# The mean of the feed-forward weights' magnitudes, taken in the course of the loop and applied in the out phase

## What is computed

```
def binarize_weight(W):
    alpha = jnp.mean(jnp.abs(W), axis=tuple(range(1, W.ndim)), keepdims=True)
    return alpha * jnp.sign(W)

xn = _layernorm(x)
ffn = einsum('bsi,oi->bso', xn, binarize_weight(weight_real)) + bias
attn: qkv = clip(xn @ Wqkv.T, -8, 8); q, k layer-normed with weights and biases;
      32 heads of 32, scores + ALiBi slopes, causal softmax, @ v, @ Wout.T
return x + attn + ffn
```

## Time and profile before

| what | value |
|---|---|
| median of 3 runs | 1423.8 us (1423.53 to 1425.67) |
| the profiled execution's own time | 1431.37 us |
| its span | 1429.6 us |
| mean granted TensorE clock | 0.987 |
| TensorE busy | 94% |
| VectorE, ScalarE, GpSimd busy | 55%, 36%, 29% |

### The profile page before, as it was taken

How to read it: one execution, slowest core, us unless ns; L and a number is a source line. 1 busy time by engine, 2 the same in 40 slices (tenths; PEclk the granted TensorE clock), 3 DMA queues, 4 the chain that set the end, 5 groups by cost and what they waited for, 6 DMA issues and landing times.

```text
span 1429.6 us, 36331 instructions
## 1 busy us (share of the span) xinstructions
PE 1347.4 (94%) x15016; PEld 680.6 (48%) x15016; DVE 789.9 (55%) x1790; ACT 511.0 (36%) x1018; POOL 421.2 (29%) x300
## 2 busy tenths in 40 slices
PE   3899999999999999699999999999999999879998
PEld 2455444454544444244345555555555555434443
DVE  7566266565666661122678778878778778001111
ACT  4454111111111110000057777777777777600000
POOL 5222000000000000000015555444455555545443
PEclk9899999999999999899999999999999999989999
DMA  6454122322223226522112322333223331225543
GB/s 241 155 168 148 74 52 66 74 73 66 67 66 73 66 71 154 168 84 71 56 51 75 88 79 79 92 85 91 83 78 88 85 85 48 91 67 162 152 157 118
DMA packets 143653, 137.47 MB, mean 96 GB/s; under 512 B 81952, under 2 KB 110752, under 8 KB 143328
## 3 DMA queue, kind: packets, MB, share of 16 engines
q1 hardware_dynamic: 79053, 99.02, 23.3%
q10 hardware_dynamic: 64467, 36.50, 9.7%
HBM read 92.90 MB, written 42.21 MB: 95 GB/s over the span
## 4 chain that ended last, share of the span: by engine, by line
PE 79%; DMA 10%; DVE 6%; SPq 2%; issue 1%; POOL 1%; ACT 1%; DVEq 0%; ACTq 0%; POOLq 0%
PE ps L1004 52%; PE ps L1079 6%; PE ps L1140 6%; DMA arena<-arena 6%; PE ps L1163 5%; PE ps L1168 4%; DVE ps L907 2%; PE ps L1056 2%; DMA arena<-q_scr 2%; PE ps L1143 1%; DMA r_scr<-arena 1%; SPq L353 1%; PE ps L1173 1%; DVE arena L835 1%; PE ps L993 1%
## 5 line engine op out<-in xcount | busy, mean ns | idle before, releaser
L1004 PE MATMUL ps<-arena 128*128 128x512 f16 x3584 | 796.0, 382 | 31.8 <-DVE arena L866 11.9
L1004 PEld LDWEIGHTS ps<-arena 128*128 128x128 f16 (+1 forms) x3584 | 349.6, 98 | 453.4 <-issue 20.5
L723 ACT ACTIVATE arena<-ps 128x512 f32<-128x512 f32 (+3 forms) x768 | 339.6, 498 | 151.1 <-PE ps L1143 98.4
L599 POOL TENSOR_TENSOR arena<-arena 128x2048 f32<-128x2048 f32 (+1 forms) x48 | 201.8, 4204 | 391.0 <-ACT arena L723 388.6
L907 DVE CUSTOM_DVE_ANT_0 ps<-ps,arena 128x128 f32<-128x128 f32 (+3 forms) x512 | 239.6, 519 | 59.1 <-PE ps L1079 57.0
L1140 PE MATMUL ps<-arena 128*32 128x512 f16 (+3 forms) x3072 | 255.5, 327 | 4.0 <-ACT arena L723 2.5
L1079 PE MATMUL ps<-arena 127*32 127x512 f16 (+3 forms) x3072 | 237.2, 327 | 17.3 <-DVE arena L907 12.8
L638 ACT ACTIVATE arena<-arena 128x512 f32 (+1 forms) x64 | 40.1, 628 | 486.7 <-DMA arena<-in_wqkv_t 313.7
L866 DVE TENSOR_SCALAR arena<-ps 128x1024 f32<-128x1024 f32 x48 | 58.8, 1225 | 218.5 <-PE ps L1004 189.2
L911 DVE TENSOR_REDUCE arena<-ps 128x1 f16<-128x512 f32 x256 | 162.9, 683 | 15.2 <-PE ps L1079 15.2
L1163 PE MATMUL ps<-arena 128*32 128x512 f32 (+3 forms) x1536 | 160.7, 485 | 0.5 <-issue 0.3
(11 more groups left out here) (51 smaller groups left out, 769.2 us busy)
## 6 DMA issues: line engine op xcount, KB each, us to landing
arena<-in_x SPq DMA_DIRECT2D x32, 512.0 KB, 4.9
arena<-in_wqkv_t SPq DMA_DIRECT2D x48, 256.0 KB, 3.0
arena<-k_scr ACTq DMA_DIRECT2D x39, 256.0 KB
base_scr<-arena SPq DMA_DIRECT2D x16, 512.0 KB, 2.8
v_scr<-arena SPq DMA_DIRECT2D x16, 512.0 KB, 2.9
arena<-r_scr SPq DMA_DIRECT2D x32, 256.0 KB
arena<-base_scr SPq DMA_DIRECT2D x16, 512.0 KB, 4.0
out_dram<-arena SPq DMA_DIRECT2D x16, 512.0 KB, 6.2
```

The lines of the kernel that those rows point to most:

```text
L599: nc.gpsimd.tensor_tensor(acc[:, :, at:HALF], former, p32[k % PSLOTS][:, :, 0:w], ALU.add)\
L723: nc.scalar.activation(p32[k % PSLOTS][:, j, 0:w], ps[:, TRB[x % RB], 0:w], ACT.Exp, scale=SCALE).then_inc(exp_done, 1)
L1004: ins = nc.tensor.matmul(dst[c], lhs(k, a), wparts[:, k, b, c * HALF:(c + 1) * HALF], start=(k == 0 and (a, b) == order[0]), stop=(k == KT ...
```

## The change

- The scaled mean is no longer needed in stage F. f_out is a plain copy; alpha is made once, ahead of the last f_out, sent through DRAM (`alpha_scr`) and loaded as a broadcast (`alpha_c`) behind the bias; POOL multiplies base by it in the new `resid(t)`.
- DVE takes magnitude and sum of a row block in a new `abs_sum(j)`: block 0 at the start, block 1 after all signs, blocks 2 to 7 in its loop, one behind each odd tile. POOL adds nothing. `split_hi` of Q waits for the block's sum, because it overwrites the raw block.
- PE: product 0 begins at the first sign and waits block by block; turn_x(2) and turn_x(3) move into products 1 and 2; two fp32 matmuls with ones stand between products 14 and 15.
- DVE's loop has xt_low(t) at its end instead of xt_low(t-1) at its start; ACT places xt_high(0) and (1) among the signs.
- First loads: x0, the transposes' identity (own semaphore `idh_ld`), x1, all eight weight blocks, x2, x3, two halves for Q, the other constants; the four broadcasts for the layer norms go to the end of the loop.
- ACT performs one Sign on a single column at the very start.
- End: POOL takes the residuals of tiles 0 and 1 ahead of the last two norms and that of tile 2 between them; DVE does c_out(0) ahead of the last reciprocals; SP issues load_base(2) ahead of the last sums_out, and store_out(0) behind it.

The core of the diff:

```
-            for t in range(2):
-                load_x(t, t, 0)
-            for dst, src in ((idh, ident_h), (idb.bitcast(U16), ident_b), (mnat.bitcast(U16), mask_nat),
-                             (mtr.bitcast(U16), mask_tr)):
-                sp.dma_start(dst, src).then_inc(const_ld, 16)
+            load_x(0, 0, 0)
+            sp.dma_start(idh, ident_h).then_inc(idh_ld, 16)
+            load_x(1, 1, 0)
             for j in range(KT):
-                sp.dma_start(wf[j], wffn_t[j * P:(j + 1) * P, :]).then_inc(wf_ld[j], 16)
-                if j == KT // 2 - 1:
-                    load_x(2, 0, 1)
+                sp.dma_start(wf[:, j, :], wffn_t[j * P:(j + 1) * P, :]).then_inc(wf_ld[j], 16)
+            load_x(2, 0, 1)
+            load_x(3, 1, 1)
             for t in range(2):
                 load_w(Q, t, t, 0)
-            for dst, src in ((ln_w["q"], q_w), (ln_b["q"], q_b), (ln_w["k"], k_w), (ln_b["k"], k_b)):
-                sp.dma_start(dst, src.partition_broadcast(P)).then_inc(bc_ld, 16)
+            for dst, src in ((idb.bitcast(U16), ident_b), (mnat.bitcast(U16), mask_nat), (mtr.bitcast(U16), mask_tr)):
+                sp.dma_start(dst, src).then_inc(const_ld, 16)
             load_w(Q, 2, 0, 1)
-            load_x(3, 1, 1)
...
             load_w(Q, NT - 1, 1, NT // 2 - 1)
+            for dst, src in ((ln_w["q"], q_w), (ln_b["q"], q_b), (ln_w["k"], k_w), (ln_b["k"], k_b)):
+                sp.dma_start(dst, src.partition_broadcast(P)).then_inc(bc_ld, 16)
             for t in range(NT - 4, NT):
                 store_base(t, t % 2)
+            sp.wait_ge(alpha_set, 1)
+            sp.dma_start(alpha_scr.rearrange("(o n) -> o n", o=1), alpha[0:1, :]).then_inc(alpha_st, 16)
...
             sp.dma_start(bias, ffn_bias.partition_broadcast(P)).then_inc(bias_ld, 16)
+            sp.dma_start(alpha_c, alpha_scr.partition_broadcast(P)).then_inc(bias_ld, 16)
+            load_base(2, 0)
             sums_out(blk_no(GROUPS - 1, 1))
             recips_in(blk_no(GROUPS - 1, 1))
-            for t in range(2, NT):
+            store_out(0, 0)
+            for t in range(3, NT):
                 load_base(t, t % 2)
                 store_out(t - 2, t % 2)
...
+            def resid(t):
                 p = t % 2
                 pool.wait_ge(base_ld[p], 32 * (t // 2 + 1))
+                nc.gpsimd.tensor_tensor(basec[p], basec[p], alpha_c, ALU.mult).then_inc(scaled, 1)
+                pool.wait_ge(scaled, t + 1)
                 nc.gpsimd.tensor_tensor(basec[p], basec[p], xres[p], ALU.add).then_inc(xres_done, 1)
                 pool.wait_ge(xres_done, t + 1)
                 nc.gpsimd.tensor_tensor(basec[p], basec[p], bias, ALU.add).then_inc(resid_done, 1)
+            pool.wait_ge(bias_ld, 32)
+            for t in range(2):
+                resid(t)
+            o_norm(GROUPS - 1, 0)
+            o_low(GROUPS - 1, 0)
+            resid(2)
+            o_norm(GROUPS - 1, 1)
+            o_low(GROUPS - 1, 1)
+            for t in range(3, NT):
+                resid(t)
...
                 act.wait_ge(w_ld[p], j * 16 + (16 * KT * (blk - 1) + 16))
+                if blk == Q:
+                    act.wait_ge(asum_done, j + 1)
...
+            act.wait_ge(ones_set, 1)
+            nc.scalar.activation(table, ones[:, 0:1], ACT.Sign)
             for t in range(2):
                 normalize_x(t, t, 0)
             for j in range(KT):
                 act.wait_ge(wf_ld[j], 16)
-                nc.scalar.activation(wsl[F][:, j, 0, :], wf[j], ACT.Sign).then_inc(sign_done, 1)
-            xt_high(0, 0)
+                nc.scalar.activation(wsl[F][:, j, 0, :], wf[:, j, :], ACT.Sign).then_inc(sign_done, 1)
+                if j == 2:
+                    xt_high(0, 0)
+                if j == 4:
+                    xt_high(1, 1)
+            normalize_x(2, 0, 1)
             for t in range(2):
                 split_hi(Q, t, t, 0)
-            with act.Fori(1, NT // 2) as j:
...
+            split_hi(Q, 2, 0, 1)
+            with act.Fori(1, NT // 2 - 1) as j:
+                for t, p, m in ((j * 2 + 1, 1, j), (j * 2 + 2, 0, j + 1)):
+                    xt_high(t - 1, 1 - p)
+                    split_hi(Q, t, p, m)
+                    normalize_x(t, p, m)
...
+            def abs_sum(j):
+                tile = wf[:, bass.ds(j, 1), :].rearrange("p o n -> p (o n)")
+                nc.vector.scalar_tensor_tensor(tile, tile, -1.0, tile, ALU.mult, ALU.max).then_inc(abs_done, 1)
+                dve.wait_ge(abs_done, j + 1)
+                dve.wait_ge(asum_done, j)
+                nc.vector.tensor_tensor(asum, asum, tile, ALU.add).then_inc(asum_done, 1)
+
+            def f_step(t, p, m, last=False):
                 if last:
+                    split_lo(Q, t, p, m)
                 else:
+                    ahead = m + 1 if p else m
+                    dve.wait_ge(x_ld[1 - p], ahead * 16 + 16)
+                    statistics(t + 1, 1 - p, lambda: split_lo(Q, t, p, m))
                 x_low(t, p)
+                f_out(t - 2, p, m - 1)
+                xt_low(t, p)
+                if p and not last:
+                    abs_sum(m + 1)
...
             xt_low(0, 0)
+            dve.wait_ge(sign_done, 1)
+            nc.vector.scalar_tensor_tensor(asum, wf[:, 0, :], -1.0, wf[:, 0, :], ALU.mult, ALU.max).then_inc(asum_done, 1)
+            dve.sem_inc(abs_done, 1)
+            xt_low(1, 1)
+            dve.wait_ge(sign_done, KT)
+            abs_sum(1)
+            dve.wait_ge(x_ld[0], 32)
+            statistics(2, 0, lambda: None)
+            dve.wait_ge(x_ld[1], 32)
+            statistics(3, 1, lambda: None)
             for t in range(2):
                 split_lo(Q, t, t, 0)
+            x_low(2, 0)
+            f_out(0, 0, 0)
+            xt_low(2, 0)
+            split_lo(Q, 2, 0, 1)
+            with dve.Fori(1, NT // 2 - 1) as j:
+                for t, p, m in ((j * 2 + 1, 1, j), (j * 2 + 2, 0, j + 1)):
+                    f_step(t, p, m)
+            f_step(NT - 1, 1, NT // 2 - 1, last=True)
+            f_out(NT - 2, 0, NT // 2 - 1)
             dve.wait_ge(alpha_sum, 1)
+            nc.vector.tensor_scalar(alpha, banks(4, 2), 1.0 / (DM * SX), None, ALU.mult)\
               .then_inc(alpha_set, 1)
...
+            f_out(NT - 1, 1, NT // 2 - 1)
...
+            c_out_step(0, 0)
             recips(GROUPS - 1, 1)
-            c_out_step(0, 0)
...
             for t in range(2):
                 turn_x(t, t)
-            pe.wait_ge(sign_done, KT)
-            f_product(0, 0)
+            pe.wait_ge(sign_done, 1)
+            f_product(0, 0, lambda k: pe.wait_ge(sign_done, k + 2))
+            f_product(1, 1, lambda k: turn_x(2, 0) if k == KT - 2 else None)
+            f_product(2, 0, lambda k: turn_x(3, 1) if k == KT - 3 else None)
+            with pe.Fori(1, NT // 2 - 1) as j:
+                for t, p in ((j * 2 + 1, 1), (j * 2 + 2, 0)):
+                    turn_x(t + 1, 1 - p)
+                    f_product(t, p)
             pe.wait_ge(ones_set, 1)
+            pe.wait_ge(asum_done, KT)
             for c in range(2):
+                ins = nc.tensor.matmul(ps[:, 4 + c, :], ones, asum[:, c * HALF:(c + 1) * HALF], start=True, stop=True)
             ins.then_inc(alpha_sum, 1)
+            f_product(NT - 1, 1)
```

More of the change, by code:

```diff
@@ L102, in build_program @@
                for s in range(2)]; at += 2 * KT * DM
-        wf = [f32(START + KT * TOK + KT * DM + j * DM, DM) for j in range(KT)]
+        wf = f32(START + KT * TOK + KT * DM, KT * DM).rearrange("p (k n) -> p k n", k=KT)
         stage = [f32(at + s * HALF, HALF) for s in range(2)]; at += 2 * HALF
-        asum = [f32(at, DM)]; at += DM
+        asum = f32(at, DM); at += DM
         xc = [f32(at + s * DM, DM) for s in range(2)]; at += 2 * DM
@@ L164, in build_program @@
         bias = f32(ln_at + 2 * DM, DM)
+        alpha_c = f32(ln_at + 3 * DM, DM)
         wo = wsl[0]
@@ L176, in build_program @@
         minus = [small[:, 51 + s:52 + s] for s in range(2)]
+        table = small[:, 53:54]
         ps = ctx.enter_context(nc.psum_tensor("ps", [P, 8, HALF], F32))
@@ L218, in build_program @@
         abs_done = sem("abs_done")
-        asump_done = sem("asump_done")
-        asumv_done = sem("asumv_done")
+        asum_done = sem("asum_done")
+        alpha_st = sem("alpha_st")
+        scaled = sem("scaled")
         alpha_sum = sem("alpha_sum")
@@ L551, in _ @@
                 f_step(t, t)
-            for j in range(1, KT // 2):
-                pool.wait_ge(abs_done, j + 1)
-                if j > 1:
-                    pool.wait_ge(asump_done, j - 1)
-                nc.gpsimd.tensor_tensor(asum[0], wf[0] if j == 1 else asum[0], wf[j], ALU.add)\
-                  .then_inc(asump_done, 1)
             with pool.Fori(1, NT // 2) as i:
@@ L614, in _ @@
                             o_low(n - 1, 1)
-            for qb in range(2):
-                o_norm(GROUPS - 1, qb)
-                o_low(GROUPS - 1, qb)
-            pool.wait_ge(bias_ld, 16)
```

(21 more changed lines are left out.)

62 lines of the change are left out of this document (12 added, 50 removed).

## The result

The changed kernel takes 1410.9 us, the median of five runs (1407.21 to 1414.71), against 1423.8 us before. The ratio is 0.991, with a 95% interval of 0.988 to 0.994: a gain of 12.9 us, where 16.0 were forecast. The 1423.8 is here the median of five runs of the kernel before, with the same lowest and highest as given above. The profiled execution took 1414.06 us, 17.3 less than that of the kernel before (1431.37).

What follows compares the result with a forecast made beforehand. TensorE, busy 94% of the span, was taken to bound the kernel, leaving its idle and slow time to win. Start 4.6 plus end 11.4 made 16.0 us off 1423.8: 1407.8 us, own range 1404 to 1412, stated range 1401 to 1416.

Steps and rivals of the forecast that it cites:

- The start's term: Stage F: sums and waits leave TensorE's path, less new waits and sums' matmuls; net gain 4.6 us, bounds 1.5 to 8.
- The end part: Out phase: early residuals let product 2 follow product 1 at once; gain 11.4 us, bounds 9.6 to 11.5.
- The new wait: Stage F loop: ScalarE's Q split waits for the block's sum; 1.04 us per pair, 5.2 us over five turns.
- What comes next: Start: VectorE's order decides; signs end at 22.0 us, x_low(2) at 33.3, TensorE idles about 2.3 us before turn_x(2).
- The restart: turn_x(4): after 5.9 us idle TensorE restarts at the lower clock; product 3 ends over 9.57 us later.
- the sums' matmuls: Between products 14 and 15: two fp32 matmuls instead of four, taken at 1.8 us.
- The table load: Start: the 1.28 us load moves ahead of the statistics wait, making all first steps 1.3 us earlier.
- second table load: With Sign first, another set could be taken and a second load become due before Exp; costed at nothing.
- The wait was not absorbed: Rival, stage F loop: the new wait is absorbed, 5.2 us more and up to 3 at turn 4; about 1401; chance 0.10.
- the end did close: Rival, out phase: the end does not close, alpha_c late or POOL order delaying c_out; 1419.2 us; chance 0.08.
- the clock did not fall in the loop: Rival: loop waits keep the clock low; one half-clock tile in each of five pairs costs 39, giving 1446.8; chance 0.03.
- the start gives nothing: Rival, start: each wait also drops the clock, 8 us; start -3.4, total gain 8, 1415.8 us; chance 0.11.

Runs made afterwards that it cites:

- experiment 1: Changed kernel with the end in its old order, multiplication by alpha kept: 1427.2 us, ratio to the kernel before 1.0025.
- experiment 2: Kernel before with only the end's orders on GpSimd, VectorE and SP changed, no alpha in the out phase: 1408.5 us, ratio 0.991.
- experiment 3: Changed kernel with each row block's magnitude and addition one tile earlier, block 2 ahead of the loop: 1403.7 us, ratio 0.986.
- experiment 4: As experiment 3, but magnitude behind an odd tile and addition behind the even tile after it: 1406.5 us, ratio 0.988.
- experiment 5: Two variants of the changed kernel: x1's load ahead of the identity, or weight loads held until x1 landed; single executions 1415.1 and 1409.2 us.
- experiment 6: Changed kernel without the early Sign on one column; one execution, first Q transposes at 182.19 us against 183.68.
- experiment 8: Experiment 4 with VectorE's order at the start rewritten and x1's load ahead of the identity: 1399.3 us, ratio 0.9805 to the kernel before.

## Why the prediction was right, and where it was off

The measured 1410.9 lies in the stated range and in the forecast's own range of 1404 to 1412. That is so because the end's term, 11.4 of the 16.0 us, was right in mechanism and size. The start's term was a miss: 1.0 us where 4.6 were forecast, below its own lower bound of 1.5, and the marks of the other profiles do not separate even that from nothing. By the steps:

- **The end part** was forecast at 11.4 us and came out at 11.5; experiments 1 and 2 show that the order makes it. alpha_c landed 9.9 us after its issue (forecast: about 10), and resid(2) ended 1.0 us ahead of its forecast, both counted from product 0.
- **The new wait** is there at the place and for the reason given: five even turns released by x_low, ScalarE's split behind VectorE's addition. Experiments 3 and 4 show the reason. The size was off: I had 1.04 us per pair and 5.2 in all. It was 1.3, and from turn_x(5) to turn_x(15) 84.6 us went by where ten tiles of 7.80 make 78.0: 6.6. The operations lasted what I had taken; the two releases on this chain, from the addition to the split and from x_low to turn_x, took 0.23 and 0.24 us, where I had allowed 0.06 to 0.09.
- **"What comes next" in the start** was the other mis-sized term. It said that the signs end at 22.0; they ended at 23.2, since x1 landed at 7.2 us, where in the kernel before its statistics had begun at 6.05, which experiment 5 shows to be the queue's order and the weight loads behind it. From the eighth sign on my chain was right: 11.0 us to turn_x(2) against 11.3. turn_x(4) came at 51.59 instead of 49.8 to 50.7, after 6.4 us of idling (forecast 5.9).
- **The restart** at turn_x(4) was taken at the size of the one before (turn_x(3) 9.41 us after turn_x(2)); it was 10.34, 0.9 more. That is chance rather than the change: the old start's other two profiles have 10.43 and 9.49, the same code at turn_x(4) in experiments 1, 5 and 6 has 9.69 to 10.27.
- So the start netted 1.0 us: 2.2 less by turn_x(5), 1.4 less in the loop, and the sums' matmuls at 1.7 (forecast 1.8). My lower bound of 1.5 had room for slow restarts but not for several small delays that add up in one chain. In experiment 1, with the same start, x1 came later still (8.36) and P was 184.78, no earlier than the 184.69 before.
- **The table load** forward, which I had counted with 1.3 us, gave nothing here (experiment 6). A row shows where an operation stands; whether moving it helps is decided by whatever ends last next, here x1's statistics.
- No second table load came: the changed kernel has one, of 1.28 us, and Identity, Copy, Sign and Exp all run behind it. The Trainium skill, page "ScalarE: Activation LUTs", section "Table sets: the hidden batching unit", says that functions of one set share a load; the trace agrees, and loading for Sign first did not choose a set that lacks Exp.
- **The rivals.** The wait was not absorbed, the end did close, and the clock did not fall in the loop: five waits of up to 1.2 us (5.8 us together), 17 us apart, left it at full speed. The Trainium skill, page "TensorE: Matmul & The Clock Gate", section "A second HAM failure mode: psum-queue depth-cycling", tells of a kernel where frequent short idling made the clock swing; the measured waits do not show it, and the measurement decides. The rival "the start gives nothing" had another cause in mind, but its size for the start (-3.4) was 4.4 us off, mine 3.6.

That the median fell by 12.9 and the sum of start and end is 12.5 is agreement within the interval (8.5 to 16.8 us), and closer than the marks' own scatter allows to claim; the profiled execution's 17.3 were larger by the middle stretch alone.

## What to carry to other kernels

Work that is spread into a loop to leave the path at the start needs a place at least one tile ahead of whoever waits for it: the same two VectorE operations cost 6.6 us just ahead of their consumer, and nothing when put one and two tiles earlier. Look for the order of the last stage's queues as well as their load: most of the gain here came from letting an engine do ready work for the next product ahead of late work for a product 60 us away. And judge a change of a few microseconds by marks in the profile at the stage it touches, when an untouched stage varies by more than the change is worth, and take more than one profile of each kernel: with the same code the mark at the end of the start moved by 1.1 to 1.7 us.

## What the runs showed of the hardware

- Whether TensorE restarts at the lower clock level after an idle of 2.5 to 4 us was not fixed. After 2.49 us ahead of stage K's first product it was slow in three of twelve profiles (both of the kernel before, and experiment 8); after the same 2.49 us ahead of stage V's first product it was slow in eleven of twelve (12.22 us for 48 matmuls each time, against 10.53 at full speed). In stage F, TensorE was fast after 2.62, 2.96 and 3.04 us ahead of turn_x(2) and slow after 3.41.
- The fall can come after the idle. After 3.69 and 3.96 us ahead of turn_x(4) (experiments 3 and 4) the 16 transposes still ran at full speed, in 1.05 us, and the product behind them took 8.76 us instead of 7.07. After 5.85 us and more both were slow each time.
- A slow restart cost 1.6 to 2.6 us (9.41 to 10.43 us from one turn to the next, instead of 7.80).
- A release of one engine by another took 0.23 to 0.24 us in the loop on this path, and 0.05 us outside of it (x_low(2) ended at 34.12, turn_x(2) began at 34.17).
- In the changed kernel a 512 KB load took 3.6 us to land for x0 and 5.4 for x1, issued 0.9 us later with small and large loads around it.
